# A decoder layer on one core: later token tiles turned by the DMA queue, the causal mask added in the row maximum, row factors made on GpSimd

## The reference

```python
x = x + attention(layernorm(x))
# in attention, with H = 16 heads, DN = 128, DR = 64, DV = 128
q  = rmsnorm(x @ w_qa, q_norm_w) @ w_qb          # 384 latents -> 16 x (128 + 64)
kv = x @ w_kva                                   # 128 latents + 64 rotary key columns
k_nope, v = split(rmsnorm(kv_c, kv_norm_w) @ w_kvb)
q_rope, k_rope = rotate(q_rope), rotate(k_rope)
scores = (q . k) / sqrt(192); scores = where(tril, scores, -1e30)
out = softmax(scores) @ v @ w_o
```

## Time and profile before

| | |
|---|---|
| time, median of 3 runs | 1169.76 us (1169.22 to 1172.05) |
| profiled execution, span | 1169.4 us (its time around the span is not told apart; the median lies 0.4 us above the span) |
| PE, busy of the span | 980.4 us (84%) |
| DVE | 959.2 us (82%) |
| ACT | 678.1 us (58%) |
| POOL | 296.4 us (25%) |
| walk, first scores to last | from 161.9 us to about 858 us |

### The profile page before, as it was taken

How to read it: one execution, slowest core, us unless ns; L and a number is a source line. 1 busy time by engine, 2 the same in 40 slices (tenths; PEclk the granted TensorE clock), 3 DMA queues, 4 the chain that set the end, 5 groups by cost and what they waited for, 6 DMA issues and landing times.

```text
span 1169.4 us, 18715 instructions
## 1 busy us (share of the span) xinstructions
PE 980.4 (84%) x6106; PEld 574.0 (49%) x6124; DVE 959.2 (82%) x2669; ACT 678.1 (58%) x1449; POOL 296.4 (25%) x524
## 2 busy tenths in 40 slices
PE   0446667899999999999999999999978655559997
PEld 0234444555555555555555555555545544435553
DVE  5757749989989888989998988888868898866885
ACT  1446557667667666756666666656512676754442
POOL 1036533223223223222322222213100113221211
PEclk9769779999999999999999999999989888769999
DMA  9300003433323336334335244336363520001333
GB/s 350 139 1 1 1 8 73 75 59 71 71 59 67 66 62 142 62 64 69 65 68 138 55 68 60 64 67 140 68 218 86 168 91 19 0 1 36 84 80 91
DMA packets 217328, 90.78 MB, mean 78 GB/s; under 512 B 191496, under 2 KB 202760, under 8 KB 216720
## 3 DMA queue, kind: packets, MB, share of 16 engines
q1 hardware_dynamic: 217232, 89.58, 33.5%
HBM read 36.06 MB, written 7.34 MB: 37 GB/s over the span
## 4 chain that ended last, share of the span: by engine, by line
PE 53%; DVE 30%; ACT 6%; issue 5%; POOL 3%; DMA 3%; SPq 0%; DVEq 0%; ACTq 0%; POOLq 0%
PE bank L1930 13%; PE bank L1880 8%; PE bank L1915 6%; PE bank L1828 3%; PE bank L1859 3%; DVE arena L709 2%; PE bank L1898 2%; DVE arena L711 2%; PE bank L1901 2%; PE bank L1899 2%; PE bank L1900 2%; PE bank L1902 2%; DVE arena L791 2%; DVE arena L675 2%; DVE arena L1529 2%
## 5 line engine op out<-in xcount | busy, mean ns | idle before, releaser
L1218 ACT ACTIVATE arena<-bank,arena,scal 128x128 f32<-128x128 f32 (+3 forms) x256 | 157.7, 616 | 112.7 <-POOL arena L1059 111.6
L1930 PE MATMUL bank<-arena 128*128 128x512 f16 x768 | 179.1, 381 | 1.9 <-DVE arena L1562 1.9
L1536 DVE SCALAR_TENSOR_TENSOR arena<-arena 128x128 f16<-128x128 f32 (+3 forms) x256 | 142.2, 555 | 9.1
L1059 POOL TENSOR_TENSOR arena<-arena,scal 128x1 f32<-128x1 f32 x256 | 51.7, 203 | 347.4 <-DVE arena L1512 345.7
L1880 PE MATMUL bank<-arena 128*128 128x512 f16 x576 | 137.6, 385 | 0.0
L1529 DVE TENSOR_SCALAR arena<-arena 128x128 f16<-128x128 f32 (+3 forms) x256 | 125.4, 490 | 7.4 <-DVE arena L1521 0.8
L1512 DVE TENSOR_REDUCE arena<-bank 128x1 f32<-128x128 f32 (+3 forms) x256 | 123.7, 483 | 7.8 <-PE bank L1903 6.7
L1915 PE MATMUL bank<-arena 128*128 128x512 f16 (+3 forms) x768 | 117.7, 304 | 11.5 <-DMA arena<-arena 5.8
L1930 PEld LDWEIGHTS bank<-arena 128*128 128x128 f16 x768 | 72.9, 98 | 81.0 <-issue 4.4
L1915 PEld LDWEIGHTS bank<-arena 128*128 128x128 f16 x768 | 71.8, 99 | 63.0 <-issue 16.5
L1237 ACT ACTIVATE arena<-bank 32x512 f32<-32x512 f32 x128 | 75.3, 588 | 26.0 <-PE bank L1859 24.7
(11 more groups left out here) (201 smaller groups left out, 2049.5 us busy)
## 6 DMA issues: line engine op xcount, KB each, us to landing
arena<-in_L_attn_w_qb SPq DMA_DIRECT2D x1, 4608.0 KB, 21.6
arena<-arena SPq DMA_TRANSPOSE x272, 2.7
arena<-in_x SPq DMA_DIRECT2D x4, 1024.0 KB, 6.9
arena<-in_L_attn_w_o SPq DMA_DIRECT2D x1, 4096.0 KB, 31.9
arena<-in_fside_BxS2xS SPq DMA_DIRECT2D x4, 1024.0 KB, 8.8
arena<-in_L_ffn_w SPq DMA_DIRECT2D x8, 512.0 KB, 7.6
out<-arena SPq DMA_DIRECT2D x16, 256.0 KB, 2.3
arena<-in_x SPq DMA_DIRECT2D x12, 256.0 KB, 3.0
```

The lines of the kernel that those rows point to most:

```text
L1218: act.activation(pf(k), banks[S_BANKS[G % 3]][:, 0:n], ACT.Exp, bias=NB[:, k:k + 1], scale=sc_exp, accum_out=SUM[:, k:k + 1]).then_inc(s_e ...
L1536: dve.scalar_tensor_tensor(out=ph_part(k, 1), in0=pf(k).rearrange("p (t c) -> p t c", c=P), scalar=R4[:, k:k + 1], in1=ph_part(k, 0), op0= ...
L1930: last = pe.matmul(banks[Y_BANK][:, :], ot(gp, a, k, (q & 3) * P, P), wo(b, gp * GH + k), start=(k == 0 and n == 0), stop=(k == GH - 1 and ...
```

## The change

- PE transposes no more inside the walk: for tiles 4 to 15 the normalised rows (`turn_rows`), the rotary keys (`turn_keys`) and the latents (`turn_latents`) are turned by DMA transposes on SP's queue, between the `turn_probs` of the rows. `prep_t`, `prep_te`, `prep_t2` and `prep_out` remain for the first four tiles alone.
- The mask product is gone from `scores`. `row_max` becomes one instruction that adds a mask of 128 x 512 (zero but for the triangle) to the scores in PSUM, in place, and takes the maximum; the sign moves into the constant of `bias`.
- The product with 4096 moves from DVE to GpSimd (`row_unit`), behind the `bias` of the next row.
- On DVE, `probs_lo` comes one row later than before: in a block it stands ahead of the `probs_hi` of the row after it. Some of the other operations change places within a block.
- The buffer `PF` of rows with three key tiles gets a gap of 8 columns between the tiles.

The core of the diff:

```diff
         def pf(k):
-            return PF[:, k * (k + 1) // 2 * P:(k + 1) * (k + 2) // 2 * P]
+
+            o = (0, P, 3 * P, 6 * P + 24)[k]
+            if k == 2:
+                return PF[:, o:o + 3 * (P + 8)].rearrange("p (t c) -> p t c", c=P + 8)[:, :, 0:P]
+            return PF[:, o:o + (k + 1) * P].rearrange("p (t c) -> p t c", c=P)
...
+            def turn_rows(n):
+
+                sp.wait_ge(xn_lo, n + 1)
+                sp.wait_ge(kv_mm, n)
+                sp.dma_start_transpose(XNT.rearrange("p (a q) -> p a q", a=8), XH).then_inc(xn_in, 16)
+
+            def turn_keys(n):
+
+                sp.wait_ge(kr_made, n + 1)
+                sp.dma_start_transpose(part_kr((n >> 2) & 1, n & 3), KN).then_inc(kr_in, 16)
+
+            def turn_latents(n):
+
+                sp.wait_ge(ch_lo, n + 1)
+                sp.dma_start_transpose(part_ct((n >> 2) & 1, n & 3), CH).then_inc(ct_in, 16)
+
             load_xt(TB)
+            turn_rows(TB)
             for i in range(NPAIR):
                 for g in range(8):
+                    if i % 2 == 1 and g == 6 and i // 2 + 5 < NT:
+                        turn_rows(i // 2 + 5)
+                    if i % 2 == 0 and g == 2 and i // 2 + TB < NT:
+                        turn_keys(i // 2 + TB)
+                    if i % 2 == 0 and g == 3 and i // 2 + TB < NT:
+                        turn_latents(i // 2 + TB)
...
-                pool.tensor_tensor(NB[:, k:k + 1], NEGM[:, k:k + 1], sc_exp, ALU.mult).then_inc(s_bias, 1)
+                pool.tensor_tensor(NB[:, k:k + 1], ROWM[:, k:k + 1], nsc_exp, ALU.mult).then_inc(s_bias, 1)
+
+            def row_unit(G):
+
+                k = G & 3
+                pool.wait_ge(s_rc, G + 1)
+                pool.tensor_tensor(R4[:, k:k + 1], RC[:, k:k + 1], pscale, ALU.mult).then_inc(s_r4, 1)
...
+                    if not (first and g == 0):
+                        row_unit(G + g - 1)
                     if (j, g) == (0, 2):
                         if prep is not None:
...
-                act.activation(pf(k), banks[S_BANKS[G % 3]][:, 0:n], ACT.Exp, bias=NB[:, k:k + 1], scale=sc_exp,
+                act.activation(pf(k), banks[S_BANKS[G % 3]][:, 0:n].rearrange("p (t c) -> p t c", c=P), ACT.Exp, bias=NB[:, k:k + 1], scale=sc_exp,
                                accum_out=SUM[:, k:k + 1]).then_inc(s_exp, 1)
...
                 n = ((g & 3) + 1) * P
                 dve.wait_ge(s_mm, G + 1)
-                dve.tensor_reduce(NEGM[:, (g & 3):(g & 3) + 1], banks[S_BANKS[G % 3]][:, 0:n], AX.X, ALU.max,
-                                  negate=True).then_inc(s_max, 1)
+                s = banks[S_BANKS[G % 3]][:, 0:n]
+                dve.tensor_tensor_reduce(s, s, maskb[:, L - n:L], 1.0, -3e38, ALU.add, ALU.max,
+                                         ROWM[:, (g & 3):(g & 3) + 1]).then_inc(s_max, 1)
 
             def row_scale(G, g):
 
                 k = g & 3
                 dve.wait_ge(s_exp, G + 1)
                 dve.reciprocal(RC[:, k:k + 1], SUM[:, k:k + 1]).then_inc(s_rc, 1)
-                dve.wait_ge(s_rc, G + 1)
-                dve.tensor_scalar(R4[:, k:k + 1], RC[:, k:k + 1], PSCALE, None, ALU.mult).then_inc(s_r4, 1)
 
...
                 G = 8 * i
                 for g in range(8):
                     row_max(G + g, g)
-                    if (j, g) == (0, 0):
+                    if not (first and g == 0):
+                        row_scale(G + g - 1, g - 1)
+                    if (j, g) == (0, 5):
                         if not first:
-                            row_scale(G - 1, 7)
-                            probs_hi(i - 1, 7)
-                            probs_lo(G - 1, 7)
+                            out_lo(2 * i - 1)
...
+                    if not (first and g < 2):
+                        probs_lo(G + g - 2, g - 2)
+                    if not (first and g == 0):
+                        probs_hi((G + g - 1) >> 3, (g - 1) & 7)
+                    if g == 0:
+                        if not first:
                             out_lo(2 * i - 2)
                     if (j, g) == (0, 1):
-                        row_scale(G, 0)
-                        probs_hi(i, 0)
-                        probs_lo(G, 0)
...
                     if (j, g) == (0, 4):
-                        row_scale(G + 3, 3)
-                        probs_hi(i, 3)
-                        probs_lo(G + 3, 3)
                         if not last:
                             rotate(i + 1)
                         if prep is not None:
                             prep_split(prep[0])
-                    if (j, g) == (0, 5):
-                        row_scale(G + 4, 4)
-                        if not first:
-                            out_lo(2 * i - 1)
-                        probs_hi(i, 4)
-                        probs_lo(G + 4, 4)
...
             def prep_mm(n):
 
-                pe.wait_ge(xn_te, n + 1)
+                if n < TB:
+                    pe.wait_ge(xn_te, n + 1)
+                else:
+                    pe.wait_ge(xn_in, 16 * (n - TB) + 16)
...
+            def latents_turned(b):
+                if b == 0:
+                    pe.wait_ge(ct_te, TB)
+                else:
+                    pe.wait_ge(ct_in, 16 * TB * b)
...
-                pe.matmul(bank[:, 0:n], qr(j, 2, q, P), kr(bp, 1 + h, 0, n), start=False, stop=False)
-                pe.matmul(bank[:, q:n], identb[:, :], maskb[:, :], start=False, stop=True).then_inc(s_mm, 1)
+                pe.matmul(bank[:, 0:n], qr(j, 2, q, P), kr(bp, 1 + h, 0, n), start=False, stop=True).then_inc(s_mm, 1)
...
                     if (j, g) == (0, 0):
                         if started(i - 5):
                             project(i - 5, range(5, 8), None)
-                        if prep is not None:
-                            prep_t(prep[0])
                     if (j, g) == (0, 1):
...
-                    if (j, g) == (0, 6):
-                        if prep is not None:
-                            prep_t2(prep[0], i + 1)
                     if (j, g) == (0, 7):
                         values(i, 0)
```

More of the change, by code:

```diff
@@ L104, in decoder_layer @@
         RT1 = take(L)
-        PF = take(10 * P)
+        PF = take(10 * P + 24)
         PH = take(20 * P, fp16)
@@ L132, in decoder_layer @@
         small = take(40)
-        NEGM, NB, SUM, RC, R4 = (small[:, 20 + 4 * k:24 + 4 * k] for k in range(5))
+        ROWM, NB, SUM, RC, R4 = (small[:, 20 + 4 * k:24 + 4 * k] for k in range(5))
         rstd = small[:, 10:11]
@@ L1042, in _ @@
                                    pattern=[[-1, P]], channel_multiplier=1).then_inc(const_made, 1)
-            pool.affine_select(out=maskb[:, :], in_=maskb[:, :], compare_op=ALU.is_ge, fill=-1e30, base=0,
+            pool.affine_select(out=maskb[:, L - P:L], in_=maskb[:, L - P:L], compare_op=ALU.is_ge, fill=-1e30, base=0,
                                pattern=[[-1, P]], channel_multiplier=1).then_inc(const_made, 1)
@@ L1137, in _ @@
             walk(pair)
+            row_unit(8 * NPAIR - 1)
             later_pool(pool)
@@ L1180, in prep_hi @@
                 act.wait_ge(xn_made, n + 1)
-                if not (n == 0):
+                if n > TB:
+                    act.wait_ge(xn_in, 16 * (n - TB))
+                elif n > 0:
                     act.wait_ge(xn_t, n)
@@ L1471, in prep_rope @@
                 sin1 = at(ROPE, (TB + tile) * DR + DR // 2, DR // 2)
-                if not (n == 0):
+                if n > TB:
+                    dve.wait_ge(kr_in, 16 * (n - TB))
+                elif n > 0:
                     dve.wait_ge(kr_t, n)
@@ L1491, in prep_split @@
                 dve.wait_ge(cf_made, n + 1)
-                if not (n == 0):
+                if n > TB:
+                    dve.wait_ge(ct_in, 16 * (n - TB))
+                elif n > 0:
                     dve.wait_ge(ct_t, n)
+                if n > 0:
                     dve.wait_ge(cn_made, n)
@@ L1568, in pair @@
                     row_max(G + g, g)
[L1569 removed]
+                    if not (first and g == 0):
+                        row_scale(G + g - 1, g - 1)
+                    if (j, g) == (0, 5):
                         if not first:
[L1571 to L1573 removed]
+                            out_lo(2 * i - 1)
+                    if (j, g) == (1, 2):
+                        qn_lo_(2 * i + 1, 1)
+                    if (j, g) == (1, 6):
+                        if not last:
+                            qn_lo_(2 * i + 2, 0)
+                    if (j, g) == (1, 7):
+                        if ahead is not None:
+                            prep_lo(ahead)
+                    if not (first and g < 2):
[4 more added lines that the diff above has]
+                        if not first:
                             out_lo(2 * i - 2)
                     if (j, g) == (0, 1):
[L1576 to L1578 removed]
                         if started(i - 5):
@@ L1582, in pair @@
                     if (j, g) == (0, 2):
-                        row_scale(G + 1, 1)
```

(35 more changed lines are left out.)

53 lines of the change are left out of this document (14 added, 39 removed).

## The result

The changed kernel takes 1277.19 us (1276.39 to 1277.96, 4 runs) against 1170.13 us of the kernel before on the same chip: ratio 1.092, 95% interval 1.0897 to 1.0943. Its profiled execution has a span of 1275.5 us, 106.1 more than before. The forecast was 1250 in a range of 1190 to 1275: the direction and the mechanism came as described, the time lies 2 us outside.

The account below looks back on a forecast made before the run. The prediction took PE to bound the steady walk. To the profiled 1169.4 us it added 48 for longer pairs and 35 for the slow clock behind stops, 1252, stated as 1250, range 1190 to 1275.

Parts of the forecast that it names:

- PE as the bound, no gap to spare: In the steady walk PE is busy nearly throughout each pair; the turned row 3 lands only 0.9 us before values.
- the 29 us that the prediction saw leaving PE: In the walk, transposes, their wait and masks leave PE: 1.7 us per even pair with a tile, 0.44 in others.
- The chain in an even pair: From rope_mm through row 3's factor and low part to its landing: PE stands at values from 17.95 to 23.65, 5.7 us.
- the price of the low part, 0.75: On DVE in even pairs, probs_lo of row 3 was taken to last 0.75 us, ending at 20.55.
- The masked maximum: On DVE, row_max of 256 columns: 0.42 us as for a plain one, plus 0.15 for writing out the maximum.
- the lower bound: For the write-out of DVE's masked maximum: nothing, if it hides behind the next instruction; the upper bound was 0.194 us.
- the rival of a dear maximum: Masked maximum costs twice a plain one on DVE; odd pairs wait too, 12 us more, 1262 and up; chance 0.08.
- The clock: Behind PE's stops at values the clock falls to half; 15 stops lose 2.3 us each, +35 us.
- the rival of a wait without the clock: The clock stays up in most of PE's stops, as at 199.7, giving 1217 us; chance 0.2.
- The sum: Over the whole kernel: 1169.4 us, plus 48 for pairs and the end, plus 35 for the clock, 1252.
- the first six pairs +2: At the walk's start, fewer products run and PE waits already; pair 4 loses, others gain or stay: +2 us.
- The DMA turns: On SP's queue, turn_latents goes ahead of row 3's transpose in even pairs; costed at nothing and at up to 0.5 us.

Follow-up runs that it names:

- the fastest version: Changed kernel with probs_lo directly behind probs_hi, the product with 4096 on DVE, and add_y ahead of the row's two parts in even pairs: 1152.13 us, ratio 0.9842.
- e1_low_direct: Changed kernel with probs_lo directly behind its probs_hi again and the turns of keys and latents one row later on SP: 1226.94 us, ratio 1.0481.
- both parts undone: Changed kernel with probs_lo directly behind probs_hi and the product with 4096 back on DVE; in this form alone 1155.62 us, ratio 0.9881.
- e6_sum_early: Changed kernel with GpSimd's rope_sum one row earlier in even pairs: 1274.85 us, ratio 1.0893.
- e11_factor_gpsimd_first: Changed kernel with probs_lo direct, add_y early, product with 4096 kept on GpSimd, rope_sin moved behind row_unit of row 3: 1186.27 us, ratio 1.0146.
- e8_fill_stop: Changed kernel with unused PE products (26, or 22 without a tile) filling the stop at values in even pairs from pair 6: 1248.72 us, ratio 1.067.

## Why the prediction was off

**PE as the bound, no gap to spare.** As soon as row 3 was late by more than its 0.9 us of slack, PE stood: that part is right. That each product which leaves PE shortens the pair is right for the odd pairs alone: in the fastest version they shrink by the 0.44 of their masks, from 20.79 to 20.36. Even pairs with a tile shrink by 1.2 where 1.7 us were counted, those without a tile next to nothing, 19.79 against 19.81 in pair 26. PE comes earlier to its rows there and stands for another engine instead; in pair 26 of the fastest version for the exponential that frees a score bank:

```profile
733.57 0.39 PE L1900 MATMUL bank<-arena 128*128 128x512 f16 x1 [0.36 <-ACT arena L1256]
```

So of the 29 us that the prediction saw leaving PE, the fastest version has 19 to show.

**The chain in an even pair.** Right step by step, with PE 0.6 us later than forecast and the end 1.1 later. Counted from the start of pair 16 (565.02): `rope_mm` ends at 12.6 (forecast 11.92; in this pair PE had waited 0.49 us for the turned rows, in others some 0.18 for `add_y`), `rope_sin` at 16.3 (15.7), the factor is there at 16.6 (16.0), `probs_hi` at 16.7 (16.05), row 5's maximum at 18.7 (18.6), the low part ends at 21.4 (20.55), `values` starts at 24.8 (23.65). PE was ready at 18.6 (17.95), so the stop is 6.2 and not 5.7. What failed in the chain is **the price of the low part, 0.75**; it took 1.65 beside `rope_sum`. The row that the price came from had a neighbour too, `rope_sin`, but one that began 0.23 us behind it: there the low part kept its 0.75, and `rope_sin` took 1.66. The 0.90 for `prep_split`'s cast went the other way: it had been read beside `rope_sin`, and alone the cast took 0.42, so that the two errors half cancel. The prediction had seen this rivalry of DVE and GpSimd in `rope_sin` and did not look for it in its own new neighbours. A smaller term is missing as well: the turned row, issued at 586.43, lands 3.0 later, and `values` starts at 589.82, some 0.4 behind the landing, where the forecast had 0.05. In the run with the filled stop, where PE was at work until the landing, this gap does not appear: issued at 578.01, landed 3.1 later, `values` at 581.12.

By the Trainium skill, "SBUF — State Buffer", section "Terms", the pair of ports is held for a whole instruction and the loser stands. The traces agree: the low part of 584.75 ends 0.55 us behind `rope_sum`, the subtraction of 584.06 0.54 behind it, while GpSimd's operation, which had begun first, takes 1.26 or 1.38.

**The masked maximum.** Taken at the price of a plain one plus 0.15. By shape (columns: busy, mean ns of one, idle before):

```profile
L1558 DVE CUSTOM_DVE_ANT_0 bank<-bank,maskb 128x512 f32<-128x512 f32 x64 | 44.3, 692 | 1.7 <-PE bank L1906 1.5
...
L1558 DVE DVE_READ_ACCUMULATOR2_ANT arena<- 128x1 f32 x256 | 36.2, 141 | 0.0
...
L1558 DVE CUSTOM_DVE_ANT_0 bank<-bank,maskb 128x256 f32<-128x256 f32 x64 | 27.2, 425 | 1.8 <-PE bank L1906 1.8
```

The plain one in the kernel before:

```profile
L1512 DVE TENSOR_REDUCE arena<-bank 128x1 f32<-128x512 f32 x64 | 43.9, 686 | 4.3 <-PE bank L1903 3.4
...
L1512 DVE TENSOR_REDUCE arena<-bank 128x1 f32<-128x256 f32 x64 | 26.6, 415 | 1.7 <-PE bank L1903 1.7
```

At 256 columns it is 425 ns against 415, at 512 columns 692 against 686. Its accumulator read of 141 ns starts together with the reciprocal, so it costs the chain next to nothing: the lower bound was the right end, and the rival of a dear maximum is gone.

**The clock.** 35 us forecast from 15 stops of 2.3; the rows show 18 stops of 2.07, 37 us, and the filled stop gave back 28 for 13 of them. All 18 stops of the changed kernel paid, so the rival of a wait without the clock is out. The row of 2.5 us at 199.7 was thin ground for it: in the same trace PE stood 2.6 us to 245.2, and the stretch from 245.4 to 248.8 was granted 0.50. The Trainium skill, "TensorE: Matmul & The Clock Gate", section "HAM oscillation", describes a loop that waits for a transfer and pays at every turn. The changed kernel's trace agrees, 18 of 18; with the shorter stops of e1_low_direct, 6 of 8 did.

**The sum.** Without the clock's 37 us, 69 are left where 48 were forecast. By pair lengths, with the clock's half stretches taken off:

| | forecast | measured |
|---|---|---|
| nine even pairs with a tile | +36 (4.0 each) | +43 (stops of 6.2 to 7.0) |
| four even without | +15 (3.7 each) | +20 (stops of 5.4 to 5.5) |
| odd pairs from 7 | -5 | -1 |
| first six pairs | +2 | +5, and 11 of the clock |
| end of the walk and later | +0.5 | +1.4 |

No step points the wrong way; what failed is the size of three terms. With the clock and the end of the walk they make up the 23 us between the sum's 1252 and the measured span of 1275.5. The stops of the 13 steady even pairs are 0.5 to 1.3 us longer each, 12 us together; the low part's 0.9 beside `rope_sum` is the largest part of it (in pairs without a tile it took 1.65 too). The odd pairs make 4 us. And **"the first six pairs +2"** came out as 16, of which 11 are the clock's; if two of the prediction's 15 stops are taken to lie there, this is 10 us. The clock in the 13 even pairs went 4 the other way, 26 us for 30, and the end of the walk adds 1.

In the first six pairs I had said that pairs other than pair 4 gain or stay, because PE waits there anyway. But rows come late there as well, and the waits for the transpose came on top, in both kinds of pair, with 5 of the 18 slow stretches. With both parts undone these pairs are shorter than before, so it was the same cause.

The odd pairs were to gain 0.4 and gained 0.1, because the row that was to land just in time, at 18.6 for a PE that wants it at 18.7, lands at 18.7. It is issued at 354.35 in pair 7 (from 338.69) and takes 3.0; `values` starts 0.55 behind the last product, where products follow one another by 0.22:

```profile
357.19 0.38 PE L1906 MATMUL bank<-arena 128*128 128x512 f16 x1
357.74 1.79 PE L1918 MATMUL bank<-arena 128*128 128x512 f16 x12 [0.17 <-issue]
```

In the fastest version, where the row lands 2.6 us ahead of `values`, the gap is gone.

**The DMA turns.** Costed at nothing up to 0.5 us: right. The landing of row 3 is unchanged at 3.0. The version with the turns and without the masked maximum is 14 us faster than the kernel before; the gap in `PF`, the other moves within a block and the early `add_y` are in these 14 us too, and no run parts them.

## What to carry to other kernels

Where a transfer ends the chain to the bounding engine, ask of every reordering what now stands between its producer and its issue, and on which other engine's queue the producer waits; two small moves that each look covered can both sit on the same row, and undoing one then shows only a part of what the two cost. Price an operation in its new neighbourhood, and ask which of two neighbours begins first, instead of taking a price from a row with other neighbours. And judge a good idea apart from its companions: here the kernel with the turns and the mask was 15 us faster, and two moves beside them cost 122.

## What the runs showed of the hardware

- A row of 128 x 512 that DVE reads from SBUF takes two to three times as long when it begins within a wide GpSimd operation: 0.75 became 1.65 (two inputs, changed kernel), 0.69 became 1.63 (e6_sum_early), and one input 0.49 became 1.47 (e11_factor_gpsimd_first). Where DVE's row began first, it kept its 0.75 and GpSimd's operation took 1.66 instead of 1.26.
- The masked maximum costs DVE what the plain one costs (692 against 686 ns at 512 columns), and its accumulator read of 141 ns overlaps the next operation.
- In the steady pairs with a tile PE's stops of 1.73 to 1.75 us did not lower the clock (0 of 8, e11_factor_gpsimd_first), those of 2.77 to 2.79 did in 6 of 8 (e1_low_direct). Those of 4.0 us and more at `values` in the walk did always (18 of 18 in the changed kernel).
- PE's first product behind a landing that it stood for came some 0.4 us after that landing (changed kernel, pair 16); with PE at work until the landing the gap was within 0.1 us (e8_fill_stop).
